# ScalarE's rows of layer 1 read from a PSUM bank, and four of each sixteen steps' rows pass from VectorE to ScalarE

## The reference, cut to what matters

```python
h = jnp.einsum('bsd,fd->bsf', xn, W1)                                  # F = 128
pair = jax.nn.relu(h[:, :, None, :] - h[:, None, :, :] + b1)           # layer 1: S x S x 128
pair = jax.nn.relu(jnp.einsum('bijf,gf->bijg', pair, W2) + b2)         # layer 2: 64 features
sim = jnp.einsum('bijg,og->bijo', pair, W3)[..., 0] + b3[0]            # layer 3: one number
sim = sim.at[:, diag, diag].set(0.0)
_, top_idx = jax.lax.top_k(sim, 25)          # the 25 keys that a token attends to
# softmax attention over those 25 keys, 32 heads of 2; then the experts and a shared MLP
```

## Time and profile before

| | |
|---|---|
| median of 3 runs | 1682.68 us (1680.66 to 1686.21) |
| the profiled execution | 1682.04 us, span 1680.1 us |
| granted TensorE clock over the span | 0.998 |
| busy | PE 1622.9 us, DVE 1541.7, ACT 1446.2, POOL 1059.5 |
| pair stage | from the first copy of a batch at 96.3 us; 16 batches, the last one starts at 1220.0 us |

### The profile page before, as it was taken

How to read it: one execution, slowest core, us unless ns; L and a number is a source line. 1 busy time by engine, 2 the same in 40 slices (tenths; PEclk the granted TensorE clock), 3 DMA queues, 4 the chain that set the end, 5 groups by cost and what they waited for, 6 DMA issues and landing times.

```text
span 1680.1 us, 32738 instructions
## 1 busy us (share of the span) xinstructions
PE 1622.9 (97%) x9092; PEld 707.8 (42%) x9092; DVE 1541.7 (92%) x4301; ACT 1446.2 (86%) x2674; POOL 1059.5 (63%) x1009
## 2 busy tenths in 40 slices
PE   7889999999999999999999999999999999989998
PEld 6732222222222222222222222222222999978887
DVE  6887889999999999999999999999998878878786
ACT  5689999999999999999999999999999687743342
POOL 3203567777777777777777777676677532376553
PEclk9999999999999999999999999999999999999999
DMA  5512311212212121212212111111141555433332
GB/s 161 197 57 76 103 46 47 65 49 66 64 47 67 48 64 48 66 51 62 65 48 63 47 53 50 41 45 44 42 131 38 167 174 180 161 113 98 114 110 66
DMA packets 78329, 135.88 MB, mean 81 GB/s; under 512 B 22336, under 2 KB 43712, under 8 KB 78272
## 3 DMA queue, kind: packets, MB, share of 16 engines
q0 software_dynamic: 31744, 69.27, 14.7%
q1 hardware_dynamic: 46528, 65.92, 11.8%
HBM read 91.04 MB, written 39.85 MB: 78 GB/s over the span
## 4 chain that ended last, share of the span: by engine, by line
DVE 56%; PE 26%; issue 8%; ACT 2%; DVEq 1%; DMA 0%; ACTq 0%
DVE arena L1368 29%; PE ps L883 16%; PE ps L843 7%; DVE arena L1436 5%; DVE arena L1426 3%; DVE arena L1406 3%; DVE idx L1393 3%; DVE smax L1417 2%; DVE arena L1392 2%; PE ps L854 2%; DVE top L1386 2%; DVE arena L1411 1%; DVE arena L1421 1%; ACT arena L1052 1%; PE ps L900 1%
## 5 line engine op out<-in xcount | busy, mean ns | idle before, releaser
L680 POOL DMA_INDIRECT arena<-kv_rows,gidx x800 | 843.1, 1054 | 370.1 <-issue 222.5
L843 PE MATMUL ps<-arena,w2t 128*64 128x512 f32 x4096 | 945.5, 600 | 12.1 <-DVE arena L1368 6.6
L1368 DVE TENSOR_SCALAR arena<-arena 128x256 f32<-128x256 f32 x2464 | 772.6, 372 | 20.0 <-PE ps L843 17.6
L1052 ACT ACTIVATE arena<-arena 128x256 f32<-128x256 f32 x1632 | 729.1, 552 | 12.8 <-DVE arena L1358 12.8
L1065 ACT ACTIVATE arena<-ps,b 128x1024 f32<-128x1024 f32 x512 | 590.4, 1153 | 5.2 <-PE ps L843 5.2
L843 PEld LDWEIGHTS ps<-arena,w2t 128*64 128x64 f32 x4096 | 267.4, 136 | 679.0 <-issue 511.3
L854 PE MATMUL ps<-arena,w3win 128*32 128x512 f32 x2048 | 272.8, 605 | 8.3 <-DVE arena L1378 8.3
L854 PEld LDWEIGHTS ps<-arena,w3win 128*32 128x32 f32 x2048 | 40.3, 108 | 216.3 <-issue 154.3
L648 POOL DMA_INDIRECT slot_inputs<-xstage,istage x64 | 70.1, 1096 | 96.0 <-issue 59.6
L1436 DVE TENSOR_TENSOR arena<-arena 128x1152 f32<-128x1152 f32 (+4 forms) x160 | 108.6, 678 | 0.4
L743 POOL DMA_INDIRECT arena<-slot_outputs,slot_get x64 | 68.4, 1069 | 51.9 <-PE ps L883 31.9
(11 more groups left out here) (150 smaller groups left out, 1927.2 us busy)
## 6 DMA issues: line engine op xcount, KB each, us to landing
arena<-kv_rows,gidx POOLq DMA_INDIRECT x800
slot_inputs<-arena SPq DMA_DIRECT2D x16, 640.0 KB, 3.9
arena<-slot_inputs SPq DMA_DIRECT2D x40, 256.0 KB, 3.6
slot_outputs<-arena SPq DMA_DIRECT2D x40, 256.0 KB, 2.2
arena<-in_L_attn_x_dram SPq DMA_DIRECT2D x16, 256.0 KB, 3.0
xstage<-arena SPq DMA_DIRECT2D x16, 256.0 KB
xn_rows<-arena SPq DMA_DIRECT2D x16, 256.0 KB
arena<-in_L_attn_x_dram SPq DMA_DIRECT2D x8, 512.0 KB, 4.2
```

The lines of the kernel that those rows point to most:

```text
L680: pool.indirect_dma_start(out=kvg[:, h, r, :], out_offset=None, in_=kv_dram, in_offset=bass.IndirectOffsetOnAxis(ap=gidx[:, h, r:r + 1], a ...
L843: last = nc.tensor.matmul(ps_l2(s)[v * G2:(v + 1) * G2, u, :], w2t[:, :], r1[:, s % R1, 4 * u + 2 * v:4 * u + 2 * v + 2, :], start=True, s ...
L1052: last = nc.scalar.activation(r1[:, s % R1, k, :], hneg_now, ACT.Relu, bias=hb_now[:, at:at + 1])
L1368: row = nc.vector.tensor_scalar(r1[:, s % R1, k, :], hneg_now, hb_now[:, at:at + 1], 0.0, ALU.add, ALU.max)
```

## The change

Four of the 77 rows of a half batch move from VectorE to ScalarE, and the table has another shape. From batch 1 on, ScalarE copies `hneg_now` once per batch into PSUM bank 7 (`ps_hneg`), behind its rows of step 0, and its rows of steps 1 to 31 read from there. Its rows of step 0, and all of batch 0, still read SBUF. Since some steps now have only 3 rows on VectorE, pieces that stood behind rows 2, 3 and 4 go behind the last row where there are fewer.

```diff
+        ps_hneg = ps[:, 7, 0:S]
+        hneg_moved = sem("hneg_moved")
         def dve_rows(s):
-            return (5, 7, 4, 5, 4, 4, 4, 7, 3, 6, 4, 6, 4, 5, 5, 4)[s % STEPS]
+            return (4, 5, 4, 5, 4, 5, 7, 6, 4, 3, 6, 3, 5, 3, 3, 6)[s % STEPS]
                 if s == 0:
                     act.wait_ge(batch_copied, b + 1)
+                if s == 1 and not first:
+                    act.wait_ge(hneg_moved, b)
                 for k in range(dve_rows(s), STEP_ROWS):
                     at = step_rows(s)[k]
-                    last = nc.scalar.activation(r1[:, s % R1, k, :], hneg_now, ACT.Relu, bias=hb_now[:, at:at + 1])
+                    last = nc.scalar.activation(r1[:, s % R1, k, :], hneg_now if first or s == 0 else ps_hneg, ACT.Relu,
+                                                bias=hb_now[:, at:at + 1])
                 last.then_inc(r1_act, 1)
+            def move_hneg(first):
+                if first:
+                    act.wait_ge(route_done, 1)
+                nc.scalar.activation(ps_hneg, hneg_now, ACT.Copy).then_inc(hneg_moved, 1)
                 for s in range(BSTEPS):
                     h = s // STEPS
                     relu1(b, s, first)
+                    if s == 0 and not first:
+                        move_hneg(done == 1)
-                        if k == 2:
+                        if k == min(2, dve_rows(s) - 1):
                             if topk and 0 <= r < ROUNDS:
                                 topk_find(found, h, r)
                             if late and s16 == 10:
                                 fold(summed, 2)
                             if late and s16 == 11:
                                 fold(summed, 4)
-                        if k == 3:
+                        if k == min(3, dve_rows(s) - 1):
                             if late and s16 == 11:
                                 invert(summed)
-                        if k == 4:
+                        if k == min(4, dve_rows(s) - 1):
                             if late and s16 == 11:
                                 scale(summed)
```

## The result

| | before | after |
|---|---|---|
| median of 20 runs, one chip, us | 1684.62 (1680.66 to 1687.44) | 1681.88 (1676.24 to 1683.78) |
| ratio, 95% interval | | 0.9982 [0.9975, 0.9990] |
| span of the profiled execution, us | 1680.1 | 1674.5 |
| a batch, mean of batches 2 to 14, us | 75.2 | 74.85 |

The change brought 2.7 us, 0.2%, where 20 us were predicted. That is inside the 0.3% that the prediction counted as no change, and outside its range of 1655 to 1678 us.

What follows compares the result with a forecast made beforehand. VectorE was taken to set the pace at 75.2 us a batch; 73.6 (VectorE), 73.6 (ScalarE), 73.3 (TensorE) plus 0.1 gave 73.7. 14 batches gain 21 us, less 1 in batch 0: 1662.5 us, range 1655 to 1678.

Steps and rivals of the forecast that it cites:

- VectorE's part: Pair stage: VectorE loses 8 rows a batch, 2.1 us, gets back 0.5 for dependent pieces: 75.2 to 73.6 us.
- The surplus in twenty rows: VectorE: twenty rows over step bounds take 0.308 us each against 0.262; the surplus was taken as a cost of steps.
- The dependent pieces at step 11: VectorE, step 11: fold, invert and scale stand right behind each other, 0.12 us for each of 4 pairs, 0.5 a batch.
- ScalarE after: ... = 73.6 us: ScalarE's work per batch after the change, from rows, evictions, exponentials and the PSUM copy: 73.6 us against 74.3 before.
- the row price of 0.36: ScalarE: a 256-element row from PSUM costs 0.36 us, estimate from the eviction's 1.00 us; upper end 0.376.
- Estimate (b): ScalarE's row price from PSUM by a 512-element copy, 35 ns less from PSUM than from SBUF: 0.365 us.
- TensorE's 73.3: TensorE's floor per batch in the pair stage: sixteen pairs of steps at 4.58 us, 73.3 us.
- the rows' median near 515 ns: Sign at ScalarE's rows: record median near 515 ns instead of 556, with starts 0.36 us apart from step 1 on.
- I add 0.1: Pair stage: 0.1 us a batch added for lumps, as the three engines' bounds are near each other, giving 73.7 us.
- Lumps: Rival: ScalarE's longer batch start makes TensorE wait 0.7 to 1.3 us; 74.3 to 75.0 us a batch, 1670 to 1680; chance 0.20.
- The price of PSUM as a rival (0.40 us): Rival: a PSUM row costs ScalarE 0.40 us, so 77.8 us a batch, +40 us, 1723 us; chance 0.09 for slower.
- 77.9 us "by the page": ScalarE's sum per batch by the Trainium skill's price, 0.400 us a row: 77.9 us, against 73.6 by the trace.

Runs made afterwards that it cites:

- k2: The changed kernel with 75 rows on VectorE in the table instead of 73 (steps 13 and 14 with 4): 1692.63 us, 1.0034 of the kernel before.
- k1: The changed kernel, still 73 rows, with one ScalarE row less in steps 0 and 1 and one more in 6 and 7: 1670.16 us, 0.9921 of before.
- the light kernels: Kernel before, changed kernel, and changed kernel with all rows from SBUF, layer 2 making two of four products from batch 1: 1681.30, 1670.37, 1713.51 us.
- k4: The changed kernel with 74 rows on VectorE, one ScalarE row less in steps 0 and 1, one more in step 7: 1664.52 us, 0.9880 of before.
- the small kernel: Separate kernel: 48 ScalarE rows from SBUF, 48 from PSUM, 12 evictions, alone and beside VectorE: 0.399 and 0.364 us a row, 1.004 an eviction.

## Why the prediction was wrong

**VectorE's part: right.** VectorE is busy 73.2 us of a batch of 74.85, where I had 73.6; the waits of layer 3 for `take_sims` and of ScalarE for the copy are gone as described. The surplus in twenty rows, 0.308 us each, which I took for a cost of the steps, isn't one: in k2 19 rows over step bounds take 0.267 us each where they don't take turns with GpSimd's issues. The dependent pieces at step 11 do stand apart, by 0.03 us before the reciprocal and 0.15 before the product behind it. VectorE has slack, so this costs nothing.

**"ScalarE after: ... = 73.6 us": the first step that failed, a term of the sum mis-sized.** It is 74.19. The term is the row price of 0.36. It was made from the eviction's 1.00 us, a distance of starts, less a slope; by ends a row is 0.364 to 0.365 and an eviction 1.004. 106 x 0.0045 + 32 x 0.004 = 0.6 us. Estimate (b) had 0.365, and 4.5 ns a row decide here: with them the sum for ScalarE is the highest of the three engines, and VectorE's 73.6 and TensorE's 73.3 no longer matter. The sign that I named, the rows' median near 515 ns, was a wrong one too. It is 732 ns, longer than before, though the rows cost less:

```profile
L1058 ACT ACTIVATE arena<-ps,arena x852: 462/732/974, 499.9 to 1099.8; 128x256 f32<-128x256 f32 x171
```

**"I add 0.1" for lumps: the second step that failed, and by the larger factor.** It was 0.66 to 0.68 us a batch. The rival *Lumps* is what happened, in the place that it named: a longer start on ScalarE, and TensorE held there. It gave 74.3 to 75.0 us a batch, which holds the 74.85, and 1670 to 1680 us, just under the 1681.88. That its figure fits is in part luck. It had TensorE's wait lengthen the batch by itself, on top of a ScalarE of 73.6 us; in fact the late TensorE then holds ScalarE, which has few rows in steps 6 to 8, and as ScalarE sets the pace, that second wait lengthens the batch. In k1 0.65 us of TensorE's wait at the start are left and cost nothing: ScalarE has no gap.

What spoke against the rival was that the copy would come earlier against TensorE. It did, by less than was needed. TensorE at the start of the batch before the change:

```profile
620.23 1.06 PE L854 MATMUL ps<-arena,w3win 128*32 128x512 f32 x8
...
625.38 1.07 PE L854 MATMUL ps<-arena,w3win 128*32 128x512 f32 x8
```

ScalarE's first row stood 1.32 us ahead of that layer 3 (618.91 against 620.23) and stands 1.94 ahead now (618.90 against 620.84): 0.62 us earlier. But from this row to the end of the eviction of step 31 it was 4.47 us (to 622.28 + 1.10) and is 6.08 now (to 624.98): 1.61 longer. The difference is 0.99, and TensorE's loss at this place went from 625.38 - 620.23 - 4.58 = 0.57 us to 1.57.

Of the signs that the prediction named as wrong, two came: a wait of over 0.5 us for the eviction at the start of each batch (1.01), and copies still near 75 us apart. TensorE is busy 844.60 of 860 us, 98.2%, where over 98.5% was named.

**The account.** Missing are 14 x (74.85 - 73.7) = 16.1 us. 14 x (74.19 - 73.6) = 8.3 is ScalarE's own work, and 14 x (0.66 - 0.1) = 7.8 the coupling. The other 0.7 is in batches 0 and 1: +1.2 us for batch 0 (predicted +1) and +0.5 for batch 1, where 0 was predicted. For batch 0 the light kernels, in which it is unchanged, give +1.1 (74.25 and 75.36 us), though both are 1.6 us longer there than on the first chip. Batch 1 takes 73.16 and 73.13 us with the lighter start (k1, k4) instead of 73.89, and 72.72 with the light TensorE, so its 0.5 us fits the coupling at the start as well.

**The price of PSUM as a rival (0.40 us): refuted**, by the small kernel and by 77.38 against 74.17 us a batch with a light TensorE. The Trainium skill (ScalarE: Activation LUTs, section "What ACT_TABLE_LOAD costs") gives one price for an activation with a bias pointer; an estimate from its figures is 0.400 us at 256 elements. That is right to 1 ns for SBUF (0.399), and 36 ns too much for PSUM (0.364). For the eviction the same estimate is 1.04 us, where 1.004 was measured. The measurement decides. The prediction's 77.9 us "by the page" took only the rows at the page's price; with the evictions at 1.04 the estimate is 79.1 us.

## What to carry to other kernels

Here three engines were within 2% of each other; moving work off the slowest made the receiver the bound, and its price was needed to 1%. Take such a price from the ends of records in a full queue, from two places with the same instructions between them. Then walk once around the loop of buffers: where does the receiver's heaviest stretch hold another engine, and where does its lightest stretch run into that engine's delay? Moving rows from the first to the second (four a batch) cost nothing here and gave back 0.6 us a batch.

## What the runs showed of the hardware

- The same ScalarE instruction (256 elements, a bias by partition) costs 0.399 us from SBUF and 0.364 from a PSUM bank, alone and beside a busy VectorE.
- The records of one and the same eviction last 1.11 to 1.54 us within a batch, while its end comes 1.004 us behind the end of the record ahead of it. Neither length nor distance of starts is its price.
- Three chips at times ran these kernels in 1831 to 1868 us instead of 1664 to 1693, on two of them with all engines waiting together for layer 2, for up to 7.4 us (the third ran the kernel before in 1841.39 us, beside the small kernel, and left no trace of it). One of them later ran the kernel before in 1684.48 us. Ratios from such a time can't be used for a question of 1%.
- Where VectorE made 19 rows in 5.07 us without a pause (k2, four times from 320 to 1180 us), the gather issue of GpSimd that was under way took 5.40 us instead of 0.95 and ended with them. Where the rows had pauses (19 in 5.82 us, changed kernel) the issues took 0.95 to 1.05 us.
